# Node rows regrouped within 1024, six loads from one queue, and flags read at a step of 16 bytes

## The reference

```
def _L0_gnn_ref(xx_anchor, input, adj, weight):
    anchor_adj = jnp.einsum('md,de,ne->mn', xx_anchor, weight, input)
    scores = jnp.where(adj > 0, anchor_adj, NEG_PAD)
    atten = jax.nn.softmax(scores / TEMPERATURE, axis=1)
    return atten @ input
h = jnp.maximum(_layernorm(x, axis=-1), 0.0)
x = x + _L0_gnn_ref(h, L0_gnn_input, adj, L0_gnn_weight)
```

## Time and profile before

| | |
|---|---|
| median of 3 runs | 942.58 us |
| the profiled execution's own time | 940.72 us |
| its span | 938.9 us |
| TensorE (PE) busy | 917.5 us (98%) |
| VectorE (DVE) busy | 815.8 us (87%) |
| ScalarE (ACT) busy | 758.3 us (81%) |
| GpSimd (POOL) busy | 629.8 us (67%) |

### The profile page before, as it was taken

One profiled execution on the slowest core, in us unless ns is written; L12 is line 12 of the kernel. 1 busy time (PEld: TensorE's weight loads), 2 busy tenths in 40 slices (PEclk: granted clock), 3 DMA queues, 4 the chain that ended last, 5 costly groups with the idle time before them and its releaser, 6 DMA issues.

```text
span 938.9 us, 25837 instructions
## 1 busy us (share of the span) xinstructions
PE 917.5 (98%) x7611; PEld 666.5 (71%) x7611; DVE 815.8 (87%) x1668; ACT 758.3 (81%) x1517; POOL 629.8 (67%) x441
## 2 busy tenths in 40 slices
PE   6979999999999999999999999999999999999997
PEld 4357777777777777777777777777777777777776
DVE  5998888888889888898888988889888888888885
ACT  4767888888888888888888888888888888888786
POOL 4897677767667766776677767676766776677610
PEclk9989999999999999999999999999999999999999
DMA  9689999999999999999999999999999999999965
GB/s 315 209 215 261 262 253 279 264 268 266 262 262 269 269 268 250 266 275 265 257 260 276 262 267 259 264 266 269 267 263 258 269 269 270 249 269 269 265 96 98
DMA packets 351977, 239.51 MB, mean 255 GB/s; under 512 B 308816, under 2 KB 333520, under 8 KB 333520
## 3 DMA queue, kind: packets, MB, share of 16 engines
q1 hardware_dynamic: 341936, 234.47, 96.8%
q10 hardware_dynamic: 10016, 4.72, 1.8%
HBM read 160.50 MB, written 3.15 MB: 174 GB/s over the span
## 4 chain that ended last, share of the span: by engine, by line
PE 95%; DVE 2%; DMA 2%; ACT 1%; issue 0%; SPq 0%; DVEq 0%; ACTq 0%
PE ps_s L707 39%; PE ps_o L748 26%; PE ps_t L725 13%; PE ps_o L750 13%; DMA nodes_raw<-in_L_gnn_input_dram 1%; DVE probs L517 1%; PE ps_t L768 1%; PE ps_s L700 1%; PE ps_s L778 1%; DVE v L577 1%; DMA pT_dma<-split 1%; DVE split L539 0%; PE ps_o L768 0%; ACT ps_t L406 0%; ACT yT_hi L451 0%
## 5 line engine op out<-in xcount | busy, mean ns | idle before, releaser
L517 DVE CUSTOM_DVE_ANT_0 probs<-ps_s,absent 128x1024 f32<-128x1024 f32 x288 | 351.7, 1221 | 80.2 <-PE ps_s L707 72.1
L350 POOL TENSOR_SCALAR absent<-adj_i 128x2048 bf16<-128x2048 int32 x144 | 274.0, 1903 | 189.4 <-DVE chunk_max L517 178.7
L354 POOL TENSOR_SCALAR absent<-absent 128x2048 bf16<-128x2048 bf16 x144 | 276.0, 1917 | 27.7 <-POOL absent L350 27.7
L436 ACT ACTIVATE pT_hi<-ps_t 128x512 f16<-128x512 f32 x288 | 171.8, 597 | 112.1 <-PE ps_t L725 109.5
L406 ACT ACTIVATE ps_t<-probs,neg_max,exp_scale 128x512 f32<-128x512 f32 x288 | 222.9, 774 | 5.3 <-DVE neg_max L527 4.0
L707 PE MATMUL ps_s<-yT_hi,hT_hi 128*128 128x512 f16 x576 | 218.8, 380 | 0.9 <-DVE chunk_max L517 0.9
L707 PE MATMUL ps_s<-yT_lo,hT_hi 128*128 128x512 f16 x576 | 218.8, 380 | 0.0
L748 PE MATMUL ps_o<-v,pT_dma 128*128 128x256 f16 x1152 | 206.9, 274 | 0.7 <-DMA pT_dma<-split 0.7
L748 PE MATMUL ps_o<-v,pT_hi 128*128 128x256 f16 x1152 | 205.7, 273 | 1.6 <-DVE v L577 1.5
L533 DVE TENSOR_TENSOR pT_lo<-ps_t,pT_hi 128x512 f16<-128x512 f32 x288 | 196.7, 683 | 5.2 <-ACT pT_hi L436 5.2
L750 PE MATMUL ps_o<-v,pT_dma 128*128 128x128 f16 x1152 | 199.1, 220 | 0.0
(11 more groups left out here) (69 smaller groups left out, 588.2 us busy)
## 6 DMA issues: line engine op xcount, KB each, us to landing
adj_i<-in_adj_dram SPq DMA_DIRECT2D x144, 1024.0 KB, 5.2
pT_dma<-split SPq DMA_TRANSPOSE x288, 3.5
x_ln<-in_x_dram SPq DMA_DIRECT2D x48, 64.0 KB, 4.9
x_res<-in_x_dram SPq DMA_DIRECT2D x48, 64.0 KB, 4.8
out_dram<-fin ACTq DMA_DIRECT2D x48, 64.0 KB, 2.9
nodes_raw<-in_L_gnn_input_dram ACTq DMA_DIRECT2D x2, 768.0 KB, 7.5
nodes_raw<-in_L_gnn_input_dram SPq DMA_DIRECT2D x2, 768.0 KB, 10.8
w<-in_L_gnn_weight_dram SPq DMA_DIRECT2D x1, 64.0 KB, 2.6
```

The lines of the kernel that those rows point to most:

```text
L350: nc.gpsimd.tensor_scalar(absent[:, c, :], adj_i[:, c, :], 1.0, 0.0, ALU.min, ALU.max)\
L354: nc.gpsimd.tensor_scalar(absent[:, c, :], absent[:, c, :], -ABSENT, ABSENT, ALU.mult, ALU.add)\
L436: nc.scalar.activation(pT_hi[:, p % BANKS, :], ps_t[k % BANKS][:, :], ACT.Copy).then_inc(hi_done, 1)
L517: nc.vector.tensor_tensor_reduce(out=probs[:, s, j * SCORE:(j + 1) * SCORE], in0=ps_s[j % 2][:, :], in1=absent[:, c, part * SCORE:(part + ...
```

## The change

The nodes are permuted within each group of 1024: partition `p` now holds the eight consecutive nodes `8 p` to `8 p + 7` of a group, so it reads 4096 bytes in one run. Block `b` of the group holds nodes `8 p + b` for all `p`. The scores come out in that order: column `128 b + p` of a 1024-column piece belongs to node `8 p + b`. The adjacency is still loaded and converted in the original order, so the mask walks the flags in the permuted order: 128 elements at a step of 8 elements of 2 bytes, eight times over. The other input (`ps_s`) and the output (`probs`) keep their order.

The nodes now come in six parts of 512 KB, all from SyncE's queue, with `x` tiles 0 and 1 behind parts 0 and 1; the wait ahead of the adjacency loads is gone. `find_part_max` runs six times over 8 blocks instead of four times over 12. `lo_h` of the first two tiles moves behind the maxima, the turn of the 128 maxima goes to `ps_o`, and TensorE's `make_y(3)`, which writes `ps_o`, waits for it to be read.

```
+    nodes_v = nodes.rearrange("(j p b) d -> j p b d", p=P, b=BLOCKS // (N // 1024))
...
+        top_areas = [ps_t[0][:, 0:P], ps_o[:, 0:P]]
...
             sp.dma_start(w[:, :], weight).then_inc(w_in, 16)
-            for u in range(2):
-                load_x(u, u)
-            for i in range(1, PARTS, 2):
-                blocks = slice(i * PART, (i + 1) * PART)
-                sp.dma_start(nodes_raw[:, blocks, :], nodes_v[:, blocks, :]).then_inc(nodes_in[i], 16)
-            sp.wait_ge(nodes_in[PARTS - 2], 16)
+            for i in range(NODE_PARTS):
+                blocks = slice(i * NODE_PART, (i + 1) * NODE_PART)
+                sp.dma_start(nodes_raw[:, blocks, :], nodes_v[i]).then_inc(nodes_in[i], 16)
+                if i < 2:
+                    load_x(i, i)
...
                 nc.vector.tensor_tensor_reduce(
-                    out=probs[:, s, j * SCORE:(j + 1) * SCORE],
-                    in0=ps_s[j % 2][:, :], in1=absent[:, c, part * SCORE:(part + 1) * SCORE],
+                    out=probs[:, s, j * SCORE:(j + 1) * SCORE].rearrange("q (b p) -> q b p", p=P),
+                    in0=ps_s[j % 2][:, :].rearrange("q (b p) -> q b p", p=P),
+                    in1=absent[:, c, part * SCORE:(part + 1) * SCORE].rearrange("q (p b) -> q b p", p=P),
...
-            for i in range(PARTS):
+            for i in range(NODE_PARTS):
                 find_part_max(i)
-                if i == 2:
-                    for u in range(2):
-                        lo_h(u, u, ps_s[u])
...
                 .then_inc(nodes_spread, 1)
+            for u in range(2):
+                lo_h(u, u, ps_s[u])
...
-                if k in (PART_TURNS - 1, 2 * PART_TURNS - 1):
-                    make_y(k // PART_TURNS)
-            pe.wait_ge(hT_lo_done, 2)
+                if k in (3, 7):
+                    make_y(k // 4)
             pe.wait_ge(nodes_spread, 1)
             nc.tensor.transpose(top_areas[1], spread_nodes[:, :], ident[:, :]).then_inc(nodes_tops_turned, 1)
-            for k in range(2, Y_BANKS):
-                make_y(k)
+            make_y(2)
+            pe.wait_ge(nodes_top_done, 1)
+            make_y(3)
+            pe.wait_ge(hT_lo_done, 2)
```

More of the change, by code:

```diff
@@ L42, in gnn_masked_attention_kernel @@
     PER_EXP = SCORE // TURN
+    NODE_PARTS = N // 1024
+    NODE_PART = BLOCKS // NODE_PARTS
     PARTS = 4
@@ L81, in gnn_masked_attention_kernel @@
     out_v = out.rearrange("(t p) d -> t p d", p=P)
-    nodes_v = nodes.rearrange("(b p) d -> p b d", p=P)
+    nodes_v = nodes.rearrange("(j p b) d -> j p b d", p=P, b=BLOCKS // (N // 1024))
     ctx = ExitStack()
@@ L127, in gnn_masked_attention_kernel @@
         inv_sum = sb("inv_sum", [P, 2, 1], fp32)
-        part_max = sb("part_max", [P, PARTS], fp32)
+        part_max = sb("part_max", [P, NODE_PARTS], fp32)
         nodes_max = sb("nodes_max", [P, 1], fp32)
@@ L157, in gnn_masked_attention_kernel @@
         Y_BANKS = BANKS + 1
-        top_areas = [ps_t[0][:, 0:P], ps_s[0][:, 2 * P:3 * P]]
+        top_areas = [ps_t[0][:, 0:P], ps_o[:, 0:P]]
         w_in = sem("w_in")
-        nodes_in = [sem(f"nodes_in{i}") for i in range(PARTS)]
+        nodes_in = [sem(f"nodes_in{i}") for i in range(NODE_PARTS)]
         x_ln_in = [sem(f"x_ln_in{i}") for i in range(2)]
@@ L436, in hi_p @@
                 nc.scalar.activation(pT_hi[:, p % BANKS, :], ps_t[k % BANKS][:, :], ACT.Copy).then_inc(hi_done, 1)
-            for i in range(0, PARTS, 2):
-                blocks = slice(i * PART, (i + 1) * PART)
-                act.dma_start(nodes_raw[:, blocks, :], nodes_v[:, blocks, :]).then_inc(nodes_in[i], 16)
             for k in range(TURNS):
@@ L444, in _ @@
                     .then_inc(nodesT_done, 1)
-                if k == 2 * PART_TURNS - 1:
+                if k == 7:
                     for u in range(2):
@@ L615, in find_part_max @@
                 dve.wait_ge(nodes_in[i], 16)
-                nc.vector.tensor_reduce(part_max[:, i:i + 1], nodes_raw[:, i * PART:(i + 1) * PART, :], AX.XY,
+                nc.vector.tensor_reduce(part_max[:, i:i + 1], nodes_raw[:, i * NODE_PART:(i + 1) * NODE_PART, :], AX.XY,
                                         ALU.max, apply_absolute_value=True).then_inc(part_max_done, 1)
@@ L631, in _ @@
             nc.vector.tensor_reduce(w_top[:, :], top_areas[0], AX.X, ALU.max).then_inc(w_top_done, 1)
-            for i in range(PARTS):
+            for i in range(NODE_PARTS):
                 find_part_max(i)
-                if i == 2:
-                    for u in range(2):
-                        lo_h(u, u, ps_s[u])
-            dve.wait_ge(part_max_done, PARTS)
+            dve.wait_ge(part_max_done, NODE_PARTS)
             nc.vector.reduce_max(nodes_max[:, :], part_max[:, :], AX.X).then_inc(nodes_max_done, 1)
@@ L772, in _ @@
             for k in range(TURNS):
-                if k % PART_TURNS == 0:
-                    pe.wait_ge(nodes_in[k // PART_TURNS], 16)
+                if k % 2 == 0:
+                    pe.wait_ge(nodes_in[k // 2], 16)
                 if k >= 2:
```

## The result

The changed kernel takes 1077.95 us (1077.49 to 1078.83, four runs), against 942.52 us for the kernel before on the same chip: a ratio of 1.144 (95% interval 1.142 to 1.146). It is slower by 135 us. The profiled execution took 1077.49 us, with a span of 1075.7 us.

A forecast was written before the change was run, and what follows sets the result against it. TensorE was taken to bound the tiles at 18.56 us, VectorE 2.18 us behind. 195.8 us of mask growth less 73.5 absorbed leaves 122.3; 940.7 + 122.3 - 6.0 = 1057.0, expected median 1059 us; 8-in-10 range 933 to 1175.

The forecast's parts named there:

- TensorE's clock holds: Steady tiles: TensorE, busy for 89% of a 20.91 us tile, keeps its full clock, so no cost.
- the signs that were to show it: Mask 1.9 us, VectorE's score waits gone, TensorE waiting for masks and low parts, tile near 20.9 us, first yT_hi near 15.4.
- The mask's growth, the middle of 0.29 and 1.08 us: All 288 masks: flags at a 16-byte step add 0.68 us each, to 1.90 us; 195.8 us more VectorE work.
- What VectorE can absorb, 73.5 us: VectorE's waits ahead of masks, 72.1 + 1.4 us over the whole run, are used up first, leaving 122.3 us.
- The start-up, -6.0 us: Start-up: faster node load brings the first yT_hi forward; gain 6.4 us, or 3.3 at the slow rate, taken as 6.0.
- the chain after the last part: Start-up: last part ready at 11.4 us, one maximum of 1.21 us to 12.6, then first yT_hi at 15.4.
- The data rate of the nodes: Node load: with 4 KB runs it rises from 298 GB/s to 413, the old rate kept as the other end.
- The new wait ahead of make_y(3): Start-up on TensorE: it waits for nodes_top, first needed by the fourth yT_hi, 1.84 us after the first; costs nothing.
- That GpSimd waits longer for masks: GpSimd, which waited 178.7 us for masks and idles 33% of the span, waits longer; no cost in the sum.
- the free rival: Masks stay at 1.22 us or grow under 0.29, hidden; only the start-up gain counts: 936.6 us median, chance 0.31.
- The whole second turn, 2.30 us: Masks: each column takes a second turn, 1.08 us more a mask; 1174 us median, chance 0.13 for this or more.
- The fourth, no gain from the start-up: Mask step free and node load no faster, first yT_hi at 18 to 22 us; 940 to 943 us, chance 0.09.

The follow-up runs named there:

- loads_only: The changed kernel with the mask reading flags contiguously, nodes still permuted, so flags and scores don't match in order; 939.31 us, ratio 0.9975.

## Why the prediction was right

The direction, the mechanism and the place were right: the mask grows past what VectorE can spare, VectorE becomes the bound, and TensorE's clock holds. The time was forecast at 1059 and came out at 1078: a growth of 116 us was forecast, and 135 was measured. Of the signs that were to show it, the waits for scores are gone, TensorE waits for low parts (`lo_d` and the low part of h) and a tile takes 21.48 us for 20.9. That TensorE's products would wait for masks did not come: they wait one step on, for `lo_d`. Three terms of the sum were off, and partly cancelled.

*The mask's growth, the middle of 0.29 and 1.08 us.* Taken 0.68, measured 0.80: 288 x 0.12 = +35 us. The bounds held; the middle was no more than that, and that it came so near is luck: no row told 0.5 from 0.95, which the forecast itself put at 1005 and 1135 us. That the cost is there, and what it hangs on, is shown by the steps of 8, 16 and 32 bytes: 1224, 2022 and 2021 ns (medians). The figure of the Trainium skill, "Vector Engine (DVE) Microarchitecture Reference", section 5.2, which gave 0.69, is for 4-byte elements at far larger hops and is too low here; the same section says that small steps cost more than large ones. Its rule on which patterns are at full rate asks for two adjacent 4-byte words, and a step of 8 bytes at 2-byte elements, which has no adjacent elements, ran at full rate. The other page, the Trainium skill, "SBUF — State Buffer" (Door 1), fits in its rule of two hits in each 16 bytes, and is wrong in its example that 8 bf16 are a free step.

*What VectorE can absorb, 73.5 us.* A tile went from 18.56 to 21.48, with 6 x 0.80 = 4.82 more work: 1.90 us a tile was absorbed, not 1.73. Over 48 tiles that is 91 us, -17.6 us against the sum. VectorE's idle time fell from 2.18 to 0.51 us a tile, by 1.67: the listed waits, while the short gaps stayed (0.45 and 0.51). The other 0.23 is that VectorE was busy for only 20.97 - 16.38 = 4.59 us a tile more: a mask that no longer waits starts about 0.08 us before the instruction ahead of it ends, and three masks a tile had waited. With all six masks long, my count by the listed waits was near the truth. As a general rule it was wrong: I had the wait down as 0.29 us for each mask, wherever it stands. The waits stand ahead of masks 1, 3 and 5 alone, and in the run with two long masks nearly the whole of one of them is paid.

*The start-up, -6.0 us.* Measured 3.8 between the changed kernel and the run with the masks alone (4.8 if each is taken against its own kernel before), and 2.4 (1.0 to 3.7) for the loads alone. The failed step is the chain after the last part. I had one maximum of 1.21 us left after the landing; in fact the first maximum could not start before 8.19 us, because ahead of it in VectorE's list stands the statistics of x tile 1, whose load now stands behind two parts of the nodes, and from there six maxima take 6.84 us, to 15.03. I had 12.6 there. These 2.4 us are the whole miss of the first yT_hi in this trace, 17.90 for 15.4. GpSimd is a second one, which the forecast kept out of this stretch. Its conversion begins at 15.31 us, right on the chain. Where it began just after the spread it cost 0.25 us (y_bound 0.41 for 0.16), and where it began just before, in the trace of the loads alone, the first yT_hi came 2.1 us later and TensorE's clock fell behind it. The forecast asked of the clock only in the steady tiles.

*The terms that held.* In the steady stretch the granted clock was 1.00 with TensorE busy for 769.30 / 859.35 = 90%. The data rate of the nodes rose as forecast, if less, from 298 to 372 GB/s. The new wait ahead of make_y(3) cost nothing that shows. That GpSimd waits longer for masks costs nothing: VectorE waits for no flags in the steady stretch.

Put together from the measured terms: 1059 + 35 - 18 + 2 = 1078. The 91 us absorbed are themselves what the measured tile leaves over, so that the sum closes is no test of it. One figure of the prediction does not follow from its own terms: by the two load rates the free rival gives 936.2 to 939.3 us as a median, not 933.5 to 939.5.

The rival that the step is free is refuted by the run with the masks alone. The whole second turn, 2.30 us, was too dear by 0.28 us. The fourth, no gain from the start-up, is excluded by the intervals of loads_only and of the run with 512-byte runs, which both lie below 1. The one trace of loads_only, with its first yT_hi at 20.01 us and 942.04 us, does look like it; its ten times do not.

Open: why the price is 0.78 ns a column and not one whole turn of 1.05; what a step between 8 and 16 bytes costs; and what share of the start-up gain each of the six-part order, the single queue and the moved hT_lo brings.

## What to carry to other kernels

Before an access pattern is bent to make a load faster, count who reads through it: a load of some 8 us was improved here, and 288 masks paid 0.8 us each. In this mask, flags of two bytes were free up to a step of 8 bytes, two to each 16 bytes, and cost 0.80 us from 16 bytes on; check the mean of the row when another instruction or type is read so. And when listing what an engine may absorb, ask of each wait what stands behind it: a wait that sits inside a ring of engines is not slack, however idle the engine looks. And an early start-up is worth only what reaches the first tile: here an engine that shared no data with the chain, and a clock that fell after a pause, each took 1.6 to 2 us of it back in one execution.

## What the runs showed of the hardware

- VectorE's mask with a bf16 operand at a step of 2, 8, 16 and 32 bytes: 1224, 1224, 2022 and 2021 ns for 1024 columns (medians, 288 each).
- GpSimd's tensor_scalar over 2048 columns from int32 to bf16: 1.90 us in order, 3.96 us reading at a step of 32 bytes, 9.33 us writing at a step of 256 bytes. The two steps differ, so this does not compare reads with writes at one step.
- Two VectorE instructions between SBUF operands that started while GpSimd worked ended only with its instruction, to within 0.1 us. The spread of the maxima took 0.29 us when it started first (changed kernel), 1.91 us beside a pass of 1.89 (loads alone) and 9.33 us beside one of 9.29 (permuted writes). y_bound took 0.16 us where it started before GpSimd's pass (512-byte runs), 0.41 in the changed kernel and 1.19 with the loads alone. Not every one does: nodes_top, which reads PSUM, stayed at 0.29 us, and y_field, a single SBUF input of one column, at 0.15. Two kernels with the same start-up code, the changed one and the one with the loads alone, differ by 2.1 us at the first yT_hi, mostly in this way.
- TensorE's mean granted clock was 0.81 of full speed in the run with permuted writes, where TensorE was busy for 67% of the span; at 88 to 90%, in the changed kernel, it stayed full.
- In the start-up of the run with the loads alone TensorE was idle for 2.13 us and was then granted 0.50 (1.2 GHz) from 23 to 26 us; in the changed kernel, after 1.34 us, it kept 1.00. From the first yT_hi to the first mask it took 6.8 and 5.2 us.
